# Gathered sums taken three behind each group, and a group of 128 ahead of the 512 gathered columns

## The chip, the cores and the metric

The kernel runs on one core of one Trainium2 chip. The metric is the device time of one execution in microseconds; the median of three runs of the kernel before is 3914.21 us (3911.45 to 3914.72). The profile is of one further execution.

## What is computed

A graph network on 6250 nodes with 128 features and 200,000 edges, sorted by destination. First comes a graph attention layer with a feed-forward part (not touched here), then four graph convolutions with the same edges; the change lies wholly in these. Cut to them, the reference is:

```python
def _gcn_conv(x, src, dst, W, b, n_nodes):
    h = x @ W
    s, d = concatenate([src, loops]), concatenate([dst, loops])
    deg = segment_sum(ones, d);  dis = rsqrt(deg)
    out = segment_sum(h[s] * (dis[s] * dis[d])[:, None], d)
    return out + b

h = relu(_batch_norm(_gcn_conv(x, src, dst, W1, b1), g1, be1))
h = relu(_batch_norm(_gcn_conv(h, src, dst, W2, b2), g2, be2))
h = relu(_gcn_conv(h, src, dst, W3, b3))
h = _gcn_conv(h, src, dst, W3, b3)
return x + h          # 6250 x 128, f32
```

Source and destination lists `s` and `d` hold the 200,000 edges and one loop per node. The sum over edges is linear, so the kernel takes most of it as a product with a matrix of edge counts.

## The kernel before

The nodes are 49 tiles of 128 (6272, padded). An earlier stage leaves a matrix of edge counts in device memory (`adj`, in strips of 32 destinations). The stage `convolutions` runs L = 4 layers. In each:

- **Start of a layer.** ScalarE rectifies `hT` into `cv_stage`, TensorE multiplies by W into `cv_w_ps`, ScalarE scales the rows into `cv_hs`, writes them to the table `hs_tab` and keeps a bf16 part; VectorE makes two more bf16 parts, so that three bf16 matmuls give close to f32. TensorE takes the parts of each piece at once into the first group's sum (`first_group`, L2304).
- **Dense groups.** A group is 512 destinations: 49 source tiles x 3 parts = 147 matmuls of 128x512 into one PSUM bank, `cv_acc` (`group`, L2290). The counts come from SP's queue (`counts_in`, L2012) in three chunks of 16, 16 and 17 source tiles. Each chunk has one buffer, which is refilled when the group before has used it (`cnt_used`), so a group's third chunk is asked for when the group before it ends. There are DG = 11 groups of 512 (0 to 10) for tiles 0 to 43, and one narrow group of 128 destinations for tile 44, with 147 matmuls of 128x128.
- **Gathered destinations.** For the last four tiles (45 to 48) there are no counts; each node there has a list of its sources in 56 slots. GpSimd gathers source rows from `hs_tab`, one indirect DMA per slot (L2063), in 28 batches of 8 slots through a ring of RING = 3 buffers; batch n waits until batch n - 3 has been summed. VectorE sums a batch with one TENSOR_REDUCE (`add_slots`, L2110). Seven batches are one tile. When a tile is complete, TensorE transposes it into `cv_acc` (`turn_sums`, L2375).
- **Reading a sum.** VectorE's `finish_group(i)` multiplies the bank by a row of scales (L2124), adds the bias into `hT` (L2128) and takes statistics (L2129). The list `SPANS` gives the 13 sums of a layer in order; two banks alternate by the index in it. After the last `finish_group` of a layer come the batch-norm coefficients (layers 0 and 1) and the next layer.
- **Last layer.** TensorE also transposes each finished sum back (`turn_rows`, L2368), VectorE adds `x` (`add_rows`, L2190), and SP writes it out (`rows_out`, L2019 and L2022). Two buffers `cv_hs` alternate, so `add_rows(n)` waits until the output DMA of n - 2 has landed.

The order on each engine is written out by hand, with waits on semaphores. Which batches are summed where is this loop on VectorE: 2 or 3 behind each of groups 0 to 10 (0, 2, 5, 7, 10, 12, 15, 17, 20, 22, 25, 28 in running total).

```python
for i in range(NGA):
    last = finish_group(i)
    if l == L - 1 and i:
        add_rows(i - 1)
    for b in range(NBK * min(i, DG) // DG, NBK * min(i + 1, DG) // DG):
        add_slots(b)
```

Of the kernel before, what the change touches and what calls it, by code (L numbers as in the profile page):

```python
# [13 lines left out]
P = 128  # L14
# [40 lines left out]
GRP = 512  # L55
# [14 lines left out]
SPARSE = 4  # L70
T0 = NT - SPARSE
# [2 lines left out]
PER_TILE = SLOTS // SB  # L74
NBK = SPARSE * PER_TILE
RING = 3
DG = T0 * P // GRP
LW = T0 * P - DG * GRP
ND = DG + 1
SPANS = [(i * (GRP // P), GRP // P) for i in range(DG)] + [(T0, SPARSE), (DG * (GRP // P), LW // P)]  # L80
NGA = len(SPANS)
CQ = ((0, 393), (393, 392), (785, 392), (1177, 392))

# [100 lines left out]
def settle(engine, steps_taken):  # L184

    engine.sem_inc(steps_taken, 1)
# [1723 lines left out]
def convolutions(nc, t, sb, pb, sem, g):  # L1910
# [8 lines left out]
    with ExitStack() as c:  # L1919
# [7 lines left out]
        SLOT_W = (SB + 1) * D  # L1927
        slots = [sb(f"cv_slots{r}", [P, SB + 1, D], F32, c) for r in range(RING - 1)]
        slots = [a[:] for a in slots]
# [23 lines left out]
        hs_out = [sem(f"cv_hs_out{u}") for u in range(2)]  # L1953
        slots_in = [sem(f"cv_slots_in{r}") for r in range(RING)]
        cnt_in = [sem(f"cv_cnt_in{q}") for q in range(3)]
# [3 lines left out]
        out_done = [sem(f"cv_out{u}") for u in range(2)]  # L1959
# [13 lines left out]
        @block.sync  # L1973
        def _(sp):
            flag = sp.value_load(irregular[0:1, 0:1], min_val=0, max_val=1)

            for l in range(L):

                with sp.If(flag):
                    sp.wait_ge(s["split"], (l + 1) * NW + 2)  # L1980
                    settle(sp, s["tick_sp"])
                    for r in range(3):
                        sp.dma_start(parts_tab.rearrange("(t p) (r d) -> p t r d", p=P, r=3)[:, :, r, :], parts[:, r, :, :]
                                     ).then_inc(s["table_out"], 16)
                    sp.wait_ge(s["table_out"], 48 * (l + 1))
                    settle(sp, s["tick_sp"])
                    with sp.Fori(0, NCH) as i:
                        sp.wait_ge(s["chunk_over"], l * NCH + i + 1)
                        settle(sp, s["tick_sp"])
                        sp.dma_start(six[:], src_pad[ds(i * P, P)].rearrange("(p c) -> p c", c=1)).then_inc(s["idx_in"], 16)  # L1990
                        sp.dma_start(dix[:], dst_pad[ds(i * P + FRONT, P)].rearrange("(p c) -> p c", c=1)
                                     ).then_inc(s["idx_in"], 16)
                    if l == L - 1:
                        with sp.Fori(0, NB // 2) as m:
                            for u in range(2):
                                sp.wait_ge(s["sum"], 2 * m + u + 3)
                                sp.dma_start(out[ds((2 * m + u) * BW, BW), :].rearrange("(b p) d -> p b d", p=P), hs[u][:]
                                             ).then_inc(out_done[u], 16)
                        sp.wait_ge(s["sum"], NB + 2)
                        sp.dma_start(out[(NB - 1) * BW:(NT - 1) * P, :].rearrange("(b p) d -> p b d", p=P),  # L2000
                                     hs[0][:, 0:BATCH - 1, :]).then_inc(out_done[0], 16)
                        sp.dma_start(out[(NT - 1) * P:N, :], hs[0][0:N_LAST, BATCH - 1, :]).then_inc(out_done[0], 16)
                        sp.wait_ge(out_done[0], 16 * (NB // 2 + 2))
                        sp.wait_ge(out_done[1], 16 * (NB // 2))
                with sp.Else():
                    def counts_in(i, n, width, strips):
                        for q, (b0, m) in enumerate(CHUNKS):
                            if isinstance(i, int) and l == 0 and i == 0 and q == 0:
                                sp.sem_inc(cnt_in[0], 16)
                                continue  # L2010
                            sp.wait_ge(cnt_used[q], n + 1)
                            sp.dma_start(cnt[q][:, 0:width, 0:m * SUB], adj[strips, :, b0 * SUB:(b0 + m) * SUB]  # L2012
                                         .rearrange("t p s -> p t s")).then_inc(cnt_in[q], 16)

                    def rows_out(n):
                        sp.wait_ge(s["sum"], n + 1)
                        t0, w = SPANS[n]
                        full = w if t0 + w < NT else w - 1
                        sp.dma_start(out[t0 * P:(t0 + full) * P, :].rearrange("(b p) d -> p b d", p=P),  # L2019
                                     hs[n % 2][:, 0:full, :]).then_inc(out_done[n % 2], 16)  # L2020
                        if full < w:
                            sp.dma_start(out[(NT - 1) * P:N, :], hs[n % 2][0:N_LAST, full, :]).then_inc(out_done[n % 2], 16)  # L2022
                    counts_in(0, l * ND, SPG, slice(0, SPG))
                    counts_in(1, l * ND + 1, SPG, slice(SPG, 2 * SPG))
                    if l < L - 1:
                        with sp.Fori(2, DG) as i:
                            counts_in(i, l * ND + i, SPG, ds(i * SPG, SPG))
                    else:
                        for i in range(2, DG):
                            counts_in(i, l * ND + i, SPG, slice(i * SPG, (i + 1) * SPG))  # L2030
                            if i >= LATE:
                                rows_out(i - LATE)
                    counts_in(DG, l * ND + DG, LW // SUB, slice(DG * SPG, DG * SPG + LW // SUB))
                    if l == L - 1:
                        for n in range(DG - LATE, NGA):
                            rows_out(n)
                        sp.wait_ge(out_done[0], 16 * 7)
                        sp.wait_ge(out_done[1], 16 * 7)

        @block.gpsimd  # L2040
        def _(pool):
# [11 lines left out]
            with pool.Else():  # L2053
                for l in range(L):
                    for u in range(2):
                        pool.wait_ge(hs_out[u], 16 * (NW // 2) * (l + 1))
                    for b in range(NBK):
                        n, (k, i) = l * NBK + b, divmod(b, PER_TILE)
                        if n >= RING:
                            pool.wait_ge(s["slots_used"], n - RING + 1)  # L2060
                        for e in range(SB):
                            at = i * SB + e
                            nc.gpsimd.indirect_dma_start(slots[n % RING][:, e, :], None, hs_tab[:, :],  # L2063
                                                         bass.IndirectOffsetOnAxis(slot_idx[:, k, at:at + 1], 0)
                                                         ).then_inc(slots_in[n % RING], 16)

        @block.vector
        def _(dve):
# [11 lines left out]
            for l in range(L):  # L2080
# [32 lines left out]
                def finish_group(i):  # L2113
                    u, n = i % 2, l * NGA + i
                    use = l * uses[u] + i // 2
                    t0, w = SPANS[i]
                    width, at = w * P, slice(t0 * P, (t0 + w) * P)
# [64 lines left out]
                with dve.Else():  # L2182
                    def add_rows(n):
                        t0, w = SPANS[n]
                        dve.wait_ge(s["out_ps"], n + 1)
                        if n >= 2:
                            dve.wait_ge(out_done[n % 2], 16 * (n // 2))
                        else:
                            dve.wait_ge(hs_out[n], 16 * (NW // 2) * L)
                        nc.vector.tensor_tensor(hs[n % 2][:, 0:w, :], x_sb[:, t0:t0 + w, :],  # L2190
                                                w_ps[n % 2][:, 0, 0:w * D].rearrange("p (b d) -> p b d", d=D), ALU.add
                                                ).then_inc(s["sum"], 1)

                    own_rows()
                    for i in range(NGA):
                        last = finish_group(i)
                        if l == L - 1 and i:
                            add_rows(i - 1)
                        for b in range(NBK * min(i, DG) // DG, NBK * min(i + 1, DG) // DG):
                            add_slots(b)  # L2200
                    if l < L - 1:
                        last.then_inc(s["y"], 1)
                    else:
                        add_rows(NGA - 1)
# [69 lines left out]
        def _(pe):  # L2274
# [36 lines left out]
            for l in range(L):  # L2311
# [43 lines left out]
                with pe.Else():  # L2355
# [6 lines left out]
                    def turn_rows(n):  # L2362
                        t0, w = SPANS[n]
                        pe.wait_ge(s["dch"], l * NGA + n + 1)
# [13 lines left out]
                    def next_group(i):  # L2378
                        pe.wait_ge(acc_read[i % 2], l * uses[i % 2] + i // 2 + 1)
                        if SPANS[i][0] == T0:  # L2380
                            turn_sums(acc[i % 2])
# [40 lines left out]
```

## Time and profile before

| | us |
|---|---|
| median of 3 runs | 3914.21 (3911.45 to 3914.72) |
| profiled execution, whole | 3912.45 |
| its span on the core | 3910.7 |
| convolutions, from about 2350 us to the end | about 1560 |
| TensorE busy over the whole span | 3568.2 (91%) |

The profiled execution is 1.76 us below the median and lies inside the runs. Its span is 1.75 us shorter than its own time. Busy shares cover stages with different limits; for this change only the last 1560 us count, and of these the end of each of the four layers (about 2722, 3109, 3496 and 3885 us) and the stretch in which gathers and dense groups run side by side.

### The profile page before, as it was taken

The numbers are of one execution on the slowest core, as the hardware profiler recorded it, in microseconds if no ns is written. First come the engines' busy times: TensorE is split into PE (matmuls) and PEld (weight loads), VectorE is DVE, ScalarE is ACT, GpSimd is POOL, SyncE is SP. The second block draws the span as 40 slices with busy tenths as digits, with TensorE's granted clock in tenths as the row PEclk, the third lists the DMA queues.
The fourth block names the chain that finished last, engine by engine and source line by source line (L and its number), as shares of the span: only waits on it lengthen the run. The fifth ranks groups of instructions, "written<-read, shape, count | busy, mean of one in ns | idle before, by whom it ended". The sixth has DMA issues, their size and how long they took to land. (4 is left out here: it accounts for less than half of the span.)

```text
span 3910.7 us, 61608 instructions
## 1 busy us (share of the span) xinstructions
PE 3568.2 (91%) x21338; PEld 2113.7 (54%) x21338; DVE 2412.0 (62%) x3535; ACT 1880.3 (48%) x5147; POOL 2355.3 (60%) x2509
## 2 busy tenths in 40 slices
PE   5799999999999999999995889999999999989998
PEld 4566666666666666666663544444544454444444
DVE  8798888888889888888884764222422242224222
ACT  4787888888878788787882563000200020002000
POOL 2677777777777777777772003655365546544654
PEclk8798888888889888888886999999999999999999
DMA  6443333333333343333335017876887688768885
GB/s 204 128 107 106 103 107 106 106 106 104 106 105 106 103 107 106 106 107 102 107 106 92 36 30 230 249 239 187 255 251 244 184 257 253 240 192 254 254 248 172
DMA packets 497047, 606.58 MB, mean 155 GB/s; under 512 B 60201, under 2 KB 427140, under 8 KB 496478
## 3 DMA queue, kind: packets, MB, share of 16 engines
q1 hardware_dynamic: 358950, 341.00, 28.9%
q0 software_dynamic: 79968, 166.57, 17.4%
q10 hardware_dynamic: 57848, 95.46, 6.9%
q8 instruction: 151, 2.47, 0.3%
q14 instruction: 130, 1.06, 0.1%
HBM read 488.30 MB, written 116.12 MB: 155 GB/s over the span
## 5 line engine op out<-in xcount | busy, mean ns | idle before, releaser
L917 POOL DMA_INDIRECT fts<-ft_tab,src_all x1568 | 1479.5, 944 | 477.7 <-issue 477.4
L2290 PE MATMUL cv_acc<-cv_cnt,cv_parts 128*128 128x512 bf16 (+1 forms) x6468 | 1312.6, 367 | 0.0
L2290 PEld LDWEIGHTS cv_acc<-cv_cnt,cv_parts 128*128 128x128 bf16 x6468 | 616.6, 99 | 692.0
L2063 POOL DMA_INDIRECT cv_slots<-hs_tab,slot_idx x600 | 567.5, 946 | 473.0 <-issue 176.6
L954 DVE TENSOR_TENSOR ohk<-iota_ps,key_cols 128x784 bf16<-128x784 f32 x784 | 725.5, 967 | 6.1
L2124 DVE TENSOR_TENSOR cv_y<-cv_acc,dis_row 128x512 f32<-128x512 f32 (+1 forms) x52 | 34.4, 661 | 950.2 <-PE cv_acc L2290 924.4
L1047 ACT ACTIVATE dist_l<-lo_iota,low 128x128 bf16<-128x128 f16 x1960 | 593.7, 387 | 18.6 <-ACT low L1042 0.8
L1206 PE MATMUL agg_ps<-terms,oh 128*64 128x141 f32 x2744 | 530.5, 365 | 28.8 <-DVE terms L991 27.9
L1206 PEld LDWEIGHTS agg_ps<-terms,oh 128*64 128x64 f32 x2744 | 459.8, 181 | 84.1 <-DVE terms L991 71.3
L1099 ACT CAST strip<-adj_ps 128x392 bf16<-128x392 f32 x784 | 371.9, 474 | 275.2 <-PE adj_ps L1150 246.5
L1150 PE MATMUL adj_ps<-ohk,ohl 128*128 128x196 bf16 x3136 | 430.1, 262 | 0.0
L2063 POOL DMA_INDIRECT spare<-hs_tab,slot_idx x296 | 279.6, 945 | 212.1 <-issue 87.4
L968 DVE TENSOR_TENSOR prod<-ftd_ps,fts 128x780 f32<-128x780 f32 (+1 forms) x392 | 271.4, 692 | 214.2 <-DMA fts<-ft_tab,src_all 204.7
L1172 PE MATMUL ftd_ps<-win,ohdT 64*128 64x130 f32 x3136 | 313.7, 324 | 48.2 <-DVE prod L968 47.1
L1146 PE MATMUL adj_ps<-own,own_low 32*128 32x392 bf16 x784 | 269.8, 344 | 75.1 <-DVE ohk L954 46.4
L2259 ACT ACTIVATE cv_sd<-cv_mv,eps 128x1 f32<-128x1 f32 x2 | 0.6, 294 | 697.4 <-DVE cv_tmp L2210 697.4
L1150 PEld LDWEIGHTS adj_ps<-ohk,ohl 128*128 128x128 bf16 x3136 | 235.0, 101 | 180.2 <-issue 178.4
L1172 PEld LDWEIGHTS ftd_ps<-win,ohdT 64*128 64x128 f32 x3136 | 234.2, 210 | 137.1 <-DVE prod L968 71.5
L1054 ACT ACTIVATE ohl<-dist_l 128x1280 bf16<-128x1280 bf16 x196 | 248.9, 1270 | 18.4 <-ACT dist_l L1047 0.7
L991 DVE TENSOR_TENSOR terms<-fts,most_ps 128x1040 f32<-128x1040 f32 x196 | 241.1, 1230 | 10.1 <-ACT most_ps L1078 9.8
L1004 DVE TENSOR_REDUCE score<-prod 128x80 f32<-128x1040 f32 x196 | 242.4, 1237 | 6.7
L949 DVE TENSOR_TENSOR ohl<-iota_ps,low_cols 128x768 bf16<-128x768 f32 x196 | 185.8, 948 | 0.0
(287 smaller groups left out, 3271.4 us busy)
## 6 DMA issues: line engine op xcount, KB each, us to landing
cv_cnt<-adj SPq DMA_DIRECT2D x88, 2048.0 KB, 9.3
cv_cnt<-adj SPq DMA_DIRECT2D x44, 2176.0 KB, 9.3
adj<-strip ACTq DMA_DIRECT2D x196, 392.0 KB
fts<-ft_tab,src_all POOLq DMA_INDIRECT x1568
win<-ft_tab SPq DMA_DIRECT2D x196, 65.0 KB
hs_tab<-cv_hs ACTq DMA_DIRECT2D x24, 448.0 KB, 3.8
cv_slots<-hs_tab,slot_idx POOLq DMA_INDIRECT x600
agg_tab<-res SPq DMA_DIRECT2D x196, 35.2 KB
```

Of the source, the lines that this page charges most:

```text
L917: nc.gpsimd.indirect_dma_start(fts[u][:, k, :], None, ft_tab[:, :], bass.IndirectOffsetOnAxis(src_all[:, n, k:k + 1], 0)).then_inc(gathere ...
L954: nc.vector.tensor_tensor(ohk[:, k.s, at, :], key_no.unsqueeze(1).to_broadcast([P, QC, KEYS]), columns(key_cols, k)[:, at].unsqueeze(2).to ...
L968: nc.vector.tensor_tensor(by_half(prod[:]), ftd_ps[:, :, 0:n * HD].rearrange("p a (c f) -> p a c f", f=HD), by_half(fts[k.f][:]), ALU.mult ...
L1047: last = nc.scalar.activation(dist_l[:, n, :], lo_iota[:], ACT.Abs, bias=low[:, k.s, n:n + 1], scale=-1.0)
L1054: nc.scalar.activation(ohl[:, k.s, LD:NA * SC, :], dist_l[:], ACT.Relu, bias=1.0, scale=-1.0).then_inc(ohl_done, 1)
L1099: nc.scalar.copy(strip[:, k.s, :, QS * q:QS * (q + 1), :].rearrange("p t a d -> p a t d"), adj_ps[q % 2][:, 0:QS * KEYS].rearrange("p (a t ...
L1146: nc.tensor.matmul(adj_ps[q % 2][:, 0:QS * KEYS], own_low[:, P - SUB - SUB * k.u:2 * P - SUB - SUB * k.u], tile_of, start=True, stop=False)
L1150: last = nc.tensor.matmul(adj_ps[q % 2][:, a * KEYS:(a + 1) * KEYS], ohl[:, k.s, n, :], ohk[:, k.s, n, :], start=False, stop=(a == QS - 1 ...
L1172: last = nc.tensor.matmul(ftd_ps[:, half, m * HD:(m + 1) * HD], ohdT[at, k.u, (c0 + m) * P:(c0 + m + 1) * P], win[at, k.u, :], start=True, ...
L1206: nc.tensor.matmul(agg_ps[0:WD, 0:WA], oh[:, k.o, col, half, :], terms[:, k.s, n, :], start=(n == 0), stop=False)
L2063: nc.gpsimd.indirect_dma_start(slots[n % RING][:, e, :], None, hs_tab[:, :], bass.IndirectOffsetOnAxis(slot_idx[:, k, at:at + 1], 0)).then ...
L2290: last = nc.tensor.matmul(a[:, 0:width], parts[:, r, b, :], cnt[q][:, 0:width // SUB, (b - b0) * SUB:(b - b0 + 1) * SUB], start=(b == 0 an ...
```

## The change

The narrow group comes before the gathered tiles in `SPANS`, and VectorE sums three batches behind each of groups 0 to 8 and the 28th behind group 9; none behind group 10. The final waits on the two output semaphores follow the new places (the gathered tiles, with two output DMAs, now have an even index).

```diff
+PER_GROUP = 3
-SPANS = [(i * (GRP // P), GRP // P) for i in range(DG)] + [(T0, SPARSE), (DG * (GRP // P), LW // P)]
+SPANS = [(i * (GRP // P), GRP // P) for i in range(DG)] + [(DG * (GRP // P), LW // P), (T0, SPARSE)]
...
-                        sp.wait_ge(out_done[0], 16 * 7)
-                        sp.wait_ge(out_done[1], 16 * 7)
+                        sp.wait_ge(out_done[0], 16 * 8)
+                        sp.wait_ge(out_done[1], 16 * 6)
...
-                        for b in range(NBK * min(i, DG) // DG, NBK * min(i + 1, DG) // DG):
+                        for b in range(min(NBK, PER_GROUP * i), min(NBK, PER_GROUP * (i + 1))):
                             add_slots(b)
```

On TensorE, at the end of a layer that is not the last (the 512-wide rows are groups 9 and 10, the 128x128 x147 row is the narrow group, `cv_acc<-ident,spare` the turning of the gathered sums, `cv_w_ps` the next layer's products), before:

```order
L2290 MATMUL cv_acc<-cv_cnt,cv_parts 128x512 x147
L2386 REGISTER_ALU
L2386 COMPARE_AND_BRANCH
L2375 MATMUL cv_acc<-ident,spare 128x128 x4
L2290 MATMUL cv_acc<-cv_cnt,cv_parts 128x128 x147
L2355 UNCONDITIONAL_BRANCH
L2317 MATMUL cv_w_ps<-cv_W,cv_stage 128x128 x7
```

and now (all lines are one further down):

```order
L2291 MATMUL cv_acc<-cv_cnt,cv_parts 128x512 x147
L2387 REGISTER_ALU
L2387 COMPARE_AND_BRANCH
L2291 MATMUL cv_acc<-cv_cnt,cv_parts 128x128 x147
L2376 MATMUL cv_acc<-ident,spare 128x128 x4
L2356 UNCONDITIONAL_BRANCH
L2318 MATMUL cv_w_ps<-cv_W,cv_stage 128x128 x7
```

The four transposes have moved behind the narrow group. On VectorE, the end of the last layer from the multiply of group 10 on (`cv_hs<-x_sb,cv_w_ps` adds `x`), before:

```order
L2124 TENSOR_TENSOR cv_y<-cv_acc,dis_row 128x512
L2128 TENSOR_SCALAR hT<-cv_y,cv_bias 128x512
L2129 BN_STATS cv_stats<-hT 128x6
L2190 TENSOR_TENSOR cv_hs<-x_sb,cv_w_ps 128x512
L2110 TENSOR_REDUCE spare<-cv_slots 128x128
L2110 TENSOR_REDUCE cv_slots<-spare 128x128
L2110 TENSOR_REDUCE spare<-cv_slots 128x128
L2124 TENSOR_TENSOR cv_y<-cv_acc,dis_row 128x512
```

and now:

```order
L2125 TENSOR_TENSOR cv_y<-cv_acc,dis_row 128x512
L2129 TENSOR_SCALAR hT<-cv_y,cv_bias 128x512
L2130 BN_STATS cv_stats<-hT 128x6
L2191 TENSOR_TENSOR cv_hs<-x_sb,cv_w_ps 128x512
L2125 TENSOR_TENSOR cv_y<-cv_acc,dis_row 128x128
L2129 TENSOR_SCALAR hT<-cv_y,cv_bias 128x128
L2130 BN_STATS cv_stats<-hT 128x6
L2191 TENSOR_TENSOR cv_hs<-x_sb,cv_w_ps 128x512
L2125 TENSOR_TENSOR cv_y<-cv_acc,dis_row 128x512
```

The three sums behind group 10 are gone from there, the narrow sum is read next, and the gathered 512 last. TensorE in the last layer, before:

```order
L2290 MATMUL cv_acc<-cv_cnt,cv_parts 128x512 x147
L2368 MATMUL cv_w_ps<-ident,hT 128x128 x4
L2375 MATMUL cv_acc<-ident,spare 128x128 x4
L2368 MATMUL cv_w_ps<-ident,hT 128x128 x4
L2290 MATMUL cv_acc<-cv_cnt,cv_parts 128x128 x147
L2368 MATMUL cv_w_ps<-ident,hT 128x128 x5
```

and now:

```order
L2291 MATMUL cv_acc<-cv_cnt,cv_parts 128x512 x147
L2369 MATMUL cv_w_ps<-ident,hT 128x128 x4
L2291 MATMUL cv_acc<-cv_cnt,cv_parts 128x128 x147
L2369 MATMUL cv_w_ps<-ident,hT 128x128 x4
L2376 MATMUL cv_acc<-ident,spare 128x128 x4
L2369 MATMUL cv_w_ps<-ident,hT 128x128 x5
```

The last row's five transposes were four of the gathered tiles and then the narrow one; now the narrow one comes first and the four last.

## Rows read from the trace of the kernel before

**Rows 1.** Waits: waiter <- releaser: us in total, times, longest.

```profile
PE cv_acc L2375 <- DVE spare L2110: 32.3, 4, 8.2
```

**Rows 2.** Chain that ended last, layer 2: start us, us, what.

```profile
3179.12 317.29 PE cv_acc L2290 x1470
3496.43 0.70 DVE cv_y L2124
...
3502.51 2.09 DVE spare L2110
...
3505.12 10.17 PE cv_acc L2290 x147
3516.82 0.72 PE cv_w_ps L2317 x4
```

**Rows 3.** Timeline, VectorE, end of layer 2: start, us, instruction, [idle before].

```profile
3505.16 0.69 DVE L2124 TENSOR_TENSOR cv_y<-cv_acc,dis_row 128x512 f32<-128x512 f32 x1 [0.57 <-PE cv_acc L2375]
...
3506.41 0.67 DVE L2129 BATCH_NORM_STATS2 cv_stats<-hT 128x6 f32<-128x490 f32 x1
3515.32 0.29 DVE L2124 TENSOR_TENSOR cv_y<-cv_acc,dis_row 128x128 f32<-128x128 f32 x1 [8.24 <-PE cv_acc L2290]
...
3515.97 0.29 DVE L2129 BATCH_NORM_STATS2 cv_stats<-hT 128x6 f32<-128x128 f32 x1
```

**Rows 4.** Timeline, VectorE, ends of layers 0 and 1.

```profile
2721.76 0.69 DVE L2124 TENSOR_TENSOR cv_y<-cv_acc,dis_row 128x512 f32<-128x512 f32 x1 [23.41 <-PE cv_acc L2290]
...
2740.59 0.29 DVE L2124 TENSOR_TENSOR cv_y<-cv_acc,dis_row 128x128 f32<-128x128 f32 x1 [8.16 <-PE cv_acc L2290]
...
3109.33 0.69 DVE L2124 TENSOR_TENSOR cv_y<-cv_acc,dis_row 128x512 f32<-128x512 f32 x1 [23.39 <-PE cv_acc L2290]
...
3129.01 0.29 DVE L2124 TENSOR_TENSOR cv_y<-cv_acc,dis_row 128x128 f32<-128x128 f32 x1 [8.79 <-PE cv_acc L2290]
```

**Rows 5.** Windows: stretch, us, PE PEld DVE ACT POOL busy (count), PEclk, DMA, GB/s.

```profile
3505.00:3508.00 3.00, 3.00 (x30) 3.00 (x29) 1.85 (x3) 0.00 (x0) 0.00 (x0) 0.50 0.00 0
3510.00:3515.00 5.00, 5.00 (x93) 5.00 (x91) 0.00 (x0) 0.00 (x0) 0.00 (x0) 1.00 0.86 264
...
3134.00:3137.00 3.00, 2.90 (x13) 2.70 (x14) 1.44 (x4) 2.46 (x7) 0.00 (x0) 0.50 1.10 348
```

**Rows 6.** The page's DMA issues of counts: KB each, median us to landing.

```profile
cv_cnt<-adj SPq DMA_DIRECT2D x88, 2048.0 KB, 9.3
```

**Rows 7.** DMA issues from 3480 to 3540 us: the narrow group's third chunk.

```profile
cv_cnt<-adj SPq DMA_DIRECT2D x1, 544.0 KB, 4.0
```

**Rows 8.** Timeline, GpSimd: layer 2's first gather.

```profile
3171.70 0.94 POOL L2063 DMA_INDIRECT spare<-hs_tab,slot_idx  x1 [59.95 <-DMA hs_tab<-cv_hs]
```

**Rows 9.** Timeline, VectorE, layer 2, behind groups 0 and 1.

```profile
3186.93 2.16 DVE L2110 TENSOR_REDUCE cv_slots<-spare 128x128 f32<-128x1152 f32 x1 [5.32 <-DMA spare<-hs_tab,slot_idx]
3197.06 2.14 DVE L2110 TENSOR_REDUCE cv_slots<-cv_slots 128x128 f32<-128x1152 f32 x1 [7.97 <-DMA cv_slots<-hs_tab,slot_idx]
3210.88 0.69 DVE L2124 TENSOR_TENSOR cv_y<-cv_acc,dis_row 128x512 f32<-128x512 f32 x1 [11.68 <-PE cv_acc L2290]
```

**Rows 10.** Timeline, all engines, end of the last layer.

```profile
3884.92 0.60 PE L2368 MATMUL cv_w_ps<-ident,hT 128*128 128x128 f32 x4
...
3885.12 0.69 DVE L2124 TENSOR_TENSOR cv_y<-cv_acc,dis_row 128x512 f32<-128x512 f32 x1 [23.25 <-PE cv_acc L2290]
...
3896.42 0.67 DVE L2190 TENSOR_TENSOR cv_hs<-x_sb,cv_w_ps 128x512 f32<-128x512 f32 x1
...
3907.02 0.39 SPq L2022 DMA_DIRECT2D out<-cv_hs  x1
3907.45 0.38 SPq L2019 DMA_DIRECT2D out<-cv_hs  x1
```

**Rows 11.** DMA issues from 3880 to 3911 us: the output.

```profile
out<-cv_hs SPq DMA_DIRECT2D x3, 256.0 KB, 3.6
```

**Rows 12.** The page's DMA issues: the output over the whole span.

```profile
out<-cv_hs SPq DMA_DIRECT2D x11, 256.0 KB, 9.7
```

## The prediction

> **What bounds the kernel now.** I read the waits first, then the chain that ended last, then the timeline and the clock at the four layer ends. TensorE is the bound inside a layer: ten groups of 512 follow each other in 317.29 us without a gap, 31.73 us each [rows 2]. Its one wait that belongs to this change is the turning of the gathered sums, which waits for VectorE's last batch in each of the four layers, 32.3 us in all and 8.2 at the longest [rows 1]. The chain shows why it lies on the path: when group 10 ends (call that moment T; 3496.43 us in layer 2), VectorE reads the sum, then sums three batches, the last from 3502.51 for 2.09 us; only then do the last transpose and, behind it in TensorE's order, the narrow group come (10.17 us from 3505.12), and the next layer's products wait for the last read [rows 2]. The windows show a second cost. TensorE starts the narrow group at a granted clock of 0.50, the lower level (1.2 GHz), after some 8 us without work: 30 matmuls in 3 us, 100 ns each. At 1.00 (2.4 GHz) the same matmuls take 5 us for 93, 53.8 ns each [rows 5].
>
> **Layers 0 to 2, what goes and what comes.** The three batches behind group 10 go ahead of it, to a place where VectorE has more than 20 us of idle time in a group (the read of group 10 came after 23.41 us of idle in layer 0 [rows 4]). Nothing then stands between group 10 and the narrow group: its bank is that of group 9, read 31 us before. I take its 147 matmuls at 53.8 ns, because TensorE comes from an uninterrupted group at full clock: 7.9 us. The bound on the other side is the 10.17 us that it takes now [rows 2, 5].
>
> Its counts must be there. Chunks 0 and 1 are asked for when group 10 has used 16 and 32 of its 49 source tiles, 21 and 11 us before T. Chunk 2 (544 KB) is asked for at T and needed after 96 matmuls, at T + 5.2; it landed 4.0 us after its issue [rows 7]. So that hides, with 1.2 us to spare. It hid before behind the sums too, which is why the trace does not show a wait for it.
>
> Behind the narrow group, TensorE turns the four gathered tiles: four transposes of this shape took 0.60 us [rows 10]. VectorE meanwhile reads the narrow sum: from 3515.32 to 3516.26, 0.94 us [rows 3]. Then it reads the gathered 512 columns: from 3505.16 to 3507.08, 1.92 us [rows 3]. This is an addition to the path; before, it was hidden behind the narrow group. The end of the layer is now T + 7.9 + 0.94 + 1.92, with joints of 0.05, that is T + 10.8. It was T + 19.8 in layer 2 (3516.26 - 3496.43) [rows 2, 3], and by the same reading (2740.59 - 2721.76 and 3129.01 - 3109.33, plus 0.94) T + 19.8 in layer 0 and T + 20.6 in layer 1 [rows 4]. Gains: 9.0, 9.8 and 9.0, together 27.8 us.
>
> The next layer's start stays as it is in its order, and its counts are asked for some 2.5 us earlier relative to the layer's end than before, since the narrow group releases its chunks earlier. I count this at nothing; SP's queue holds nothing else there. One cost may be new: between layers 2 and 3 TensorE now idles about 3 us instead of 1.5, and might fall to the lower level, as it stands between layers 1 and 2, where 13 matmuls filled 2.90 of 3 us at 0.50 [rows 5]. At full clock they would have taken half, so at most 1.5 us, and less where ScalarE is the slower one. I take 0 and keep 1.5 for the range.
>
> The Trainium skill ("TensorE: Matmul & The Clock Gate", Part 1) states two clock levels, 1.2 GHz after idle time and 2.4 GHz after work, with 106.7 and 55.6 ns from start to start at 128 columns; the trace agrees, with 100 and 53.8 ns. By that figure the narrow group would take 8.2 us. The Trainium skill (same title, Part 4, on transposes) also says that transposes do not count as work for this gate; the four that now end a layer would then lengthen the idle time by 0.6 us, and the sum would be smaller by up to the 1.5 us of the bound above. No run here shows it yet.
>
> **Three batches behind every group.** The gathers must keep up. In layer 2 they start at 3171.70 [rows 8] = T - 324.7; the first batch was summed at 3186.93 and the second at 3197.06, both as they landed, so a batch takes 10.1 us, and a sum 2.15 us [rows 9]. Three need 30.4 us against 31.73 of a group [rows 2]. The tightest place is the first: the third batch lands at about 3207.2, its sum ends at 3209.4, and the read of group 1 is due at 3210.88 [rows 9]. If it were late, nothing would be lost until 31 us later, since group 2 uses the other bank. Later the distance grows by 1.3 us a group. The last batch lands at T - 324.7 + 15.2 + 27 x 10.1 = T - 36.8, waits for group 9 and is summed by T - 28. The transposes want it at T + 7.9, so the cover is 36 us. GpSimd already ran at this pace beside full count traffic between groups 0 and 3, and TensorE's groups there were no longer. Cost: nothing.
>
> **Last layer.** T is 3885.12 [rows 10]. The transposes of group 9 (0.60 us, from T - 0.2) come first, so the narrow group ends at T + 8.3. VectorE reads it until T + 9.2 and adds `x` to group 10 (0.67 us [rows 10]) until T + 9.9; the output of group 10 is issued and lands 3.6 us later [rows 11], at T + 13.5. Beside this run the read of the gathered 512 (to T + 11.9), the narrow output, and four transposes (to T + 12.5). The last addition needs the buffer of group 10: it is a new wait, from about T + 12.5 to T + 13.6. Then 0.67 us and two issues of 0.39 and 0.38 us [rows 10] end at T + 15.1. Before, the last issue ended at 3907.83 = T + 22.7, with 2.9 us to the span's end, and I leave that tail as it is. Gain 7.6 us. A landing of 9.7 us, the median over the whole span where transfers compete [rows 12], would make it 1.5; a landing below 2.5 us would make it 8.7. I take the value of the last 31 us, since nothing else is in flight there.
>
> **Sum.** 27.8 + 7.6 = 35.4 us. The profiled execution took 3912.45 us and would take 3877.1; the median of the runs is 1.8 us above the profiled one, so I forecast 3879 us for the median (-0.9%).
>
> **Rivals.** (A) The order helps but the clock does not: the narrow group still takes 10.2 us (10.9 in layer 1, where the half level lasted longer). That takes back 2.3, 3.0, 2.3 and 1.9 us, 9.5 in all: gain 25.9, time 3888. For: the clock fell at different distances from the start of idle time. Against: no gap is left in front of the group. (B) Chunk 2 comes late and takes the place of the wait: if it landed like the large chunks, in 9.3 us [rows 6], the narrow group would end at T + 9.3 + 51 x 0.0538 = T + 12.0, 4.1 us later in each layer: gain 19, time 3895. Against: 544 KB is a quarter of a large chunk and was measured at 4.0 alone; the gathers that ran beside it are gone. (C) The last output buffer costs 6 us more: gain 29.3, time 3885. (D) Slower: the gathers fall behind. One place, the transposes behind the narrow group, and one price: with p us for a batch the last sum ends at T - 324.7 + 5.1 + 28p + 2.15, and it decides once that passes T + 7.9 plus the gain of 9 us, at p = 11.9 us. At p = 12.5, which is 2.4 more than measured, each layer would lose 15 us net: 3914 + 60 = 3974. For: every batch now goes at this pace and the gathers get no pause. Against: the measured 10.1 is set by the issue of eight DMAs and was the same beside full count traffic. (E) The change does nothing: TensorE waits for something else at T: 3914. The order of the instructions speaks against it.
>
> **Numbers.** Forecast 0.72 (own range 3873 to 3884), A 0.09, B 0.05, C 0.07, D 0.03, E 0.02, and 0.02 for smaller losses beside E. The bound of 1.5 us and the three runs' spread of 3.3 us are in the forecast's range; widened to A and C, and to the low side because the layer starts may profit from earlier counts, it is 3870 to 3890. What counts as a change here is 0.2%, 7.8 us. Faster: 0.72 + 0.09 + 0.05 + 0.07 + 0.01 = 0.94; same 0.03; slower 0.03.
>
> **What would show it.** Right: at each layer end the narrow group starts at T at a granted clock of 1.00 and ends at T + 7.9; the wait for VectorE at L2376 is gone; the last read ends at T + 10.8; no reduce lies behind group 10; the last gather of a layer is issued more than 30 us before T. Wrong in a step: a gap near T + 5 inside the narrow group (B); a rate of 100 ns in it (A); a wait for the output DMA over 3 us in the last addition (C); TensorE waiting for a reduce at L2376 or for a late read at groups 2 or 3 (D). I would be wrong altogether if the ten groups of 512 in a layer took longer than 317 us.

## The result, and the profile after

The changed kernel takes 3877.86 us (median of 4 runs, 3875.01 to 3881.62), the kernel before 3912.83 us on the same chip (4 runs, 3910.61 to 3914.72). The ratio is 0.9911, with a 95% interval of 0.9894 to 0.9929. The forecast was 3879 us.

The table follows four stretches of the convolutions in the two profiled executions. T is VectorE's first read of group 10; "start" runs from the last read of a layer to the first read of the next one.

| us | before | after | less by |
|---|---|---|---|
| whole span | 3910.7 | 3873.5 | 37.2 |
| up to the first read of layer 0 | 2404.55 | 2401.59 | 3.0 |
| groups 0 to 10, a layer | 317.21, 317.21, 317.21, 321.13 | 317.21, 317.20, 317.20, 321.13 | 0.0 |
| T to the next layer's first read | 70.36, 69.89, 67.56 | 61.59, 61.75, 58.57 | 8.8, 8.1, 9.0 |
| of it from T to the end of the last read | 19.8, 20.6, 19.8 | 11.0, 11.0, 11.0 | 8.8, 9.6, 8.9 |
| of it the start | 50.6, 49.3, 47.7 | 50.6, 50.8, 47.6 | 0.0, -1.5, 0.1 |
| last layer, T to the end of the span | 25.6 | 17.3 | 8.3 |

So 34.2 us come from the four layer ends, and 3.0 us of this pair of executions from stages that the change doesn't touch; those moved between 2400.5 and 2410.3 us over all the profiled executions here and are chance. The medians differ by 35.0.

The chain that ended last, at the end of layer 2 (start, us, what), answers to [rows 2]:

```profile
3159.23 325.50 PE cv_acc L2291 x1617
3485.69 0.60 DVE cv_y L2125
3486.32 0.50 DVE hT L2129
3486.84 0.68 DVE cv_stats L2130
3488.07 0.72 PE cv_w_ps L2318 x4
```

The reader is to see one piece of 1617 matmuls (eleven groups of 147, the narrow one among them) where there were 1470, a break with three sums, and 147. The chain now leaves TensorE only for the read of the gathered columns. The timeline of the same moment (start, us, instruction) answers to [rows 3]:

```profile
3475.70 9.02 PE L2291 MATMUL cv_acc<-cv_cnt,cv_parts 128*128 128x512 bf16 x150
...
3476.54 0.69 DVE L2125 TENSOR_TENSOR cv_y<-cv_acc,dis_row 128x512 f32<-128x512 f32 x1 [27.75 <-PE cv_acc L2291]
...
3484.55 0.61 PE L2376 MATMUL cv_acc<-ident,spare 128*128 128x128 f32 x4
3484.75 0.29 DVE L2125 TENSOR_TENSOR cv_y<-cv_acc,dis_row 128x128 f32<-128x128 f32 x1 [6.27 <-PE cv_acc L2291]
...
3485.61 0.67 DVE L2125 TENSOR_TENSOR cv_y<-cv_acc,dis_row 128x512 f32<-128x512 f32 x1
```

The narrow sum is ready at T + 8.21, the gathered one is read from T + 9.07. The waits list has no entry for L2376 any more. The windows (stretch, us, busy PE PEld DVE ACT POOL with counts, granted clock, DMA share, GB/s) answer to [rows 5]: the narrow group at full clock, and the start of layer 2 at half of it.

```profile
3478.00:3484.00 6.00, 6.00 (x112) 6.00 (x110) 0.48 (x1) 0.00 (x0) 0.00 (x0) 1.00 0.90 284
...
3112.00:3119.00 7.00, 6.22 (x29) 5.99 (x29) 2.47 (x6) 5.50 (x12) 0.00 (x0) 0.50 1.12 356
```

The last batch of layer 2: GpSimd's last gather, and VectorE's sum of it, which ends 27.7 us before T (the first row is GpSimd's, the second VectorE's):

```profile
3431.16 0.94 POOL L2064 DMA_INDIRECT spare<-hs_tab,slot_idx  x1 [0.30 <-issue]
```

```profile
3446.67 2.12 DVE L2111 TENSOR_REDUCE spare<-spare 128x128 f32<-128x1152 f32 x1
```

In the last layer the chain shows the new wait for the buffer of group 10's output, as [rows 10] did not have:

```profile
3856.64 8.22 PE cv_acc L2291 x147
...
3865.75 0.68 DVE cv_hs L2191
...
3866.44 2.29 DMA out<-cv_hs
...
3868.82 0.69 DVE cv_hs L2191
```

The output landed in 2.29 us, and VectorE waited 0.39 us for it beyond its own work.

### The profile page after: what moved, and what is told of

The parts are those of the page before. It is cut to its first block and busy times, and to the rows that moved or that the text cites. A ratio compares the mean times of both kernels' runs of the same rounds, so it can differ in the third digit from the quotient of the medians.

```text
span 3873.5 us, 61608 instructions
## 1 busy us (share of the span) xinstructions
PE 3554.9 (92%) x21338; PEld 2105.3 (54%) x21338; DVE 2411.6 (62%) x3535; ACT 1881.1 (49%) x5147; POOL 2358.9 (61%) x2509
## 5 line engine op out<-in xcount | busy, mean ns | idle before, releaser
L2291 PEld LDWEIGHTS cv_acc<-cv_cnt,cv_parts 128*128 128x128 bf16 x6468 | 608.5, 98 | 692.4
L1147 PE MATMUL adj_ps<-own,own_low 32*128 32x392 bf16 x784 | 269.5, 344 | 76.9 <-DVE ohk L955 49.5
L2111 DVE TENSOR_REDUCE spare<-cv_slots 128x128 f32<-128x1152 f32 x43 | 91.4, 2126 | 165.1 <-DMA cv_slots<-hs_tab,slot_idx 164.9
```

Source lines behind the costliest of these rows:

```text
L1147: nc.tensor.matmul(adj_ps[q % 2][:, 0:QS * KEYS], own_low[:, P - SUB - SUB * k.u:2 * P - SUB - SUB * k.u], tile_of, start=True, stop=False)
L2291: last = nc.tensor.matmul(a[:, 0:width], parts[:, r, b, :], cnt[q][:, 0:width // SUB, (b - b0) * SUB:(b - b0 + 1) * SUB], start=(b == 0 an ...
```

## Experiments

Medians stand with their number of runs. Since the stages ahead scatter by some us from run to run, and the stretches from T on repeat within 0.2 us between executions of one kernel, the stretches are the finer measure; both are given. The order of the four numbers is always: T to the next layer's first read for layers 0, 1 and 2, and T to the end for the last. Before: 70.4, 69.9, 67.6, 25.6. Changed kernel: 61.6, 61.8, 58.6, 17.3.

### The changed kernel again, and each part alone

> The changed kernel once more, beside the others on the same chip. My theory (the three sums leave TensorE's path at each layer end, and the narrow group runs at full clock): 34 us below the kernel before, 3876 to 3881. The theory that part of the first difference was chance in the stages ahead of the convolutions (3.0 us of 37.2 in the two profiled executions): the same number, with those stages within 1 us of before.

3875.76 us (4 runs) against 3911.34 (14 runs), ratio 0.9907 (0.9892 to 0.9922). Stretches 61.6, 61.8, 58.4, 17.2. The first read of layer 0 came at 2409.17 us here and at 2401.59 in the first profile: 7.6 us of chance in the stages ahead, so the 3.0 us above can be that. The expectation that these stages stay within 1 us of the kernel before did not hold: they were 4.6 us later here. It is the four stretches that repeat.

The order alone:

```diff
-                        for b in range(min(NBK, PER_GROUP * i), min(NBK, PER_GROUP * (i + 1))):
+                        for b in range(NBK * min(i, DG) // DG, NBK * min(i + 1, DG) // DG):
```

> Only the narrow group is moved ahead of the gathered tiles; the sums stay spread 2 or 3 behind groups 0 to 10, three of them behind group 10. Theory 1 (the order alone is enough): these three end at T + 8.2, just when the narrow group ends, so they hide behind it; the last read ends at T + 11.0 to 11.5 as in the changed kernel, the time is 3878 to 3881. Theory 2 (the earlier sums carry the gain): the transposes still wait for VectorE, the layer end stays near T + 17 or later, time 3900 or more.

3878.44 us (5 runs), ratio 0.9913 (0.9899 to 0.9926). Stretches 61.7, 61.9, 58.6, 17.6, that is 0.6 us more than the changed kernel in all. Its timeline at the end of layer 2, with T at 3475.66:

```profile
3481.89 2.15 DVE L2111 TENSOR_REDUCE spare<-spare 128x128 f32<-128x1152 f32 x1
3483.67 0.75 PE L2376 MATMUL cv_acc<-ident,spare 128*128 128x128 f32 x4
3483.96 0.28 DVE L2125 TENSOR_TENSOR cv_y<-cv_acc,dis_row 128x128 f32<-128x128 f32 x1
```

The last of the three sums ends at T + 8.4, the narrow group at T + 8.2. The narrow sum is read 0.1 us later than in the changed kernel there and in layer 0, and 0.35 to 0.4 us later in layer 1 and in the last layer, where the three sums end at T + 8.6 and T + 9.1. Theory 1 stands, and the earlier sums add next to nothing to the new order.

The sums alone, in the kernel before:

```diff
+PER_GROUP = 3
-                        for b in range(NBK * min(i, DG) // DG, NBK * min(i + 1, DG) // DG):
+                        for b in range(min(NBK, PER_GROUP * i), min(NBK, PER_GROUP * (i + 1))):
```

> Only the sums are moved (three behind each group, none behind group 10); the gathered tiles stay ahead of the narrow group. Theory 1 (either part alone removes the wait, and this one has the shorter tail, since the small sum is read last): the four transposes take 0.5 us at T, the narrow group ends at T + 8.7, the last read at T + 9.7 against T + 11.0 in the changed kernel; in the last layer the last output is 64 KB and waits for no buffer, about 2 us better. Gain 41 us, time 3871 to 3874, below the changed kernel. Theory 2 (the order is what matters): no better than 3878, or the wait at L2375 remains.

3871.93 us (4 runs), ratio 0.9901 (0.9886 to 0.9916). Stretches 60.7, 59.6, 57.8, 15.8: 5.3 us less than the changed kernel. Its timeline at the end of layer 2, with T at 3474.09:

```profile
3473.89 0.60 PE L2376 MATMUL cv_acc<-ident,spare 128*128 128x128 f32 x4
...
3474.84 8.38 PE L2291 MATMUL cv_acc<-cv_cnt,cv_parts 128*128 128x128 bf16 x147 [0.35 <-DVE cv_y L2125]
...
3483.25 0.29 DVE L2125 TENSOR_TENSOR cv_y<-cv_acc,dis_row 128x128 f32<-128x128 f32 x1 [5.41 <-PE cv_acc L2291]
```

The transposes stand ahead of the narrow group and cost 0.95 us there (with a wait of 0.35 us for the other bank), but the last read is the short one: it starts at T + 9.2 and ends at T + 10.1, against T + 11.0. The forecast of T + 9.7 left out the wait for the bank, which is read only after T. Of the 5.3 us, 2.6 are this earlier end of the last read in layers 0 to 2 (0.87 us each), 1.45 are the last layer, and 1.3 are the start of layer 2 (49.5 us here, 50.8 in the changed kernel), which no run explains.

It was run once more beside the changed kernel:

> The kernel with only the sums moved, once more, beside the changed kernel on one chip. Theory 1 (its tail is shorter by 1.3 us in each of three layers and by 1.5 us in the last): 4 to 6 us below the changed kernel. Theory 2 (the difference in the first runs was chance): the same time within 2 us.

> The changed kernel as the partner of the run before it: 3876 to 3880, 34 us below the kernel before, both theories.

3873.75 us (4 runs) against 3874.65 (4 runs) of the changed kernel: 0.9 us, and not the 4 to 6 of theory 1. Stretches 60.7, 59.6, 57.8, 15.9 against 61.6, 61.8, 58.6, 17.2: again 5.3 us less in the trace. Over both pairs of runs the medians are 3872.5 and 3875.2 us (8 runs each). In whole times the difference is inside the scatter of the stages ahead; the difference in the trace repeats to 0.1 us. By the trace this is the best kernel here; whole times do not separate the two.

### The clock by itself

In the kernel before, the idle time is filled (FILL = 33) and nothing else is changed:

```diff
                         for k in range(SPARSE):
+                            if k == SPARSE - 1:
+                                for f in range(FILL):
+                                    nc.tensor.matmul(w_ps[0][:, 1, :], parts[:, 0, 0, :],
+                                                     parts[:, 0, 0:4, :].rearrange("p b d -> p (b d)"), start=True, stop=True)
                             pe.wait_ge(s["slots_used"], l * NBK + (k + 1) * PER_TILE)
```

> The kernel before, with 33 matmuls of 128x512 into an unused PSUM bank while TensorE waits for the last gathered sum (7.1 us of the 8.2 us wait). Nothing is taken off the path; only the idle time is filled. Theory 1 (the granted clock carries part of the gain): the narrow group runs at 1.00 and takes 8.2 us in place of 10.2, 10.9, 10.2 and 9.6, gain 8 us, time 3905. Theory 2 (the clock is a reading without an effect on the time, and the whole gain is the wait): 3913, no change. If the filler itself is late it can only add up to 1 us a layer.

3901.93 us (10 runs), ratio 0.9977 (0.9968 to 0.9986), 9.4 us below before. Stretches 67.6, 68.7, 66.1, 23.8: 7.2 us less. The narrow group behind the filler, in the timeline and by windows:

```profile
3493.44 7.07 PE L2377 MATMUL cv_w_ps<-cv_parts 128*128 128x512 bf16 x32
...
3501.59 8.37 PE L2291 MATMUL cv_acc<-cv_cnt,cv_parts 128*128 128x128 bf16 x147
```

```profile
3496.00:3500.00 4.00, 4.00 (x20) 1.84 (x19) 3.93 (x3) 0.00 (x0) 0.00 (x0) 1.00 0.18 65
3502.00:3507.00 5.00, 5.00 (x93) 5.00 (x91) 1.64 (x3) 0.00 (x0) 0.00 (x0) 1.00 0.27 67
```

The clock stays at 1.00 through the wait, and the narrow group takes 8.4 us in place of 10.2. The wait itself is as long as before. The narrow groups alone gave back 8.3 us in the four layers; the layer starts took 1.0 of it again. So of the 34 us about 7 are the clock, and some 27 the wait, after what the read of the gathered columns adds to the path; theory 2 falls.

### How far the gathers were from their limit

GpSimd gets small extra work behind each batch, four or eight iotas (PAD):

```diff
+                        for e in range(PAD):
+                            nc.gpsimd.iota(iota[:], [[1, P]], base=0, channel_multiplier=0,
+                                           allow_small_or_imprecise_dtypes=True).then_inc(padded, 1)
+                            pool.wait_ge(padded, n * PAD + e + 1)
```

> The changed kernel with four small iotas on GpSimd behind each batch of gathers, each waited for, so that a batch takes longer (about 11.3 us in place of 10.1; p is read from the trace). Theory 1 (the gathers have a cover of 36 us, used up only at p = 11.4 for the transposes at T + 8.2, with the last sum at T - 317.5 + 28p): no group and no layer end moves, T to the next layer's first read stays 61.6, 61.8, 58.6 and 17.3 us. Theory 2 (the pace is already at its limit, since VectorE waits for the landing of nearly every batch): each 1.2 us shows in full, 28 x 1.2 = 34 us a layer, over 100 us in all.

One run, 3876.92 us; stretches 61.6, 61.7, 58.7, 17.2, nothing moved. The pace went from 10.0 to 11.35 us a batch (11.5 in the mean of layer 2, since two batches took longer). The last sum of layer 2, with T at 3478.07, ends 1.0 us before T where it ended 27.7 us before T in the changed kernel:

```profile
3474.91 2.13 DVE L2117 TENSOR_REDUCE spare<-spare 128x128 f32<-128x1152 f32 x1 [7.35 <-DMA spare<-hs_tab,slot_idx]
```

> The same with eight iotas, p about 12.5 us. Theory 1: now beyond the point. The last sum ends at about T' - 317.5 + 28p with T' the end of group 10 had nothing moved, T' + 32.5 at p = 12.5, so each layer is 24 us longer than in the changed kernel and the whole about 97 us longer (about 3975, above the kernel before). Some groups of 512 wait for a bank, since VectorE reads them late. Theory 2 (pace at its limit from the start): twice the cost of the run with four iotas. Theory 3 (GpSimd's pace does not matter): 3878.

One run, 3986.36 us, above the kernel before. At 12.6 us a batch (12.7 in the mean of layer 2), the last sum of layer 2 ends here:

```profile
3570.86 2.08 DVE L2117 TENSOR_REDUCE spare<-spare 128x128 f32<-128x1152 f32 x1 [12.42 <-DMA spare<-hs_tab,slot_idx]
```

Group 0 was read at 3220.08 and would have been followed by T 317.2 us later, at 3537.3; the sum ends 35.7 us behind that. TensorE also waits for banks that VectorE reads late, in the waits list (waiter, releaser, us, times, longest):

```profile
PE cv_acc L2297 <- DVE cv_y L2131: 51.2, 11, 8.8
```

From the first read of one layer to that of the next it is 28.1, 27.4 and 28.1 us more than in the changed kernel, and 22.3 in the last layer, 106 in all against 97 expected; the expectation counted 12.5 us a batch, and 0.1 us more for each of 28 batches is 2.8 us a layer. Theory 1 stands on these two runs: no cost at 11.35 us a batch, and nearly the full price at 12.6, so the point lies between. That VectorE waits for the landing of 72 of the 112 batches in the changed kernel costs nothing.

### A late third chunk

```diff
+                            if q == 2 and width < SPG:
+                                sp.dma_start(cnt[q][:, 0:SPG, 0:m * SUB], adj[DG * SPG:DG * SPG + SPG, :, b0 * SUB:(b0 + m) * SUB]
+                                             .rearrange("t p s -> p t s")).then_inc(cnt_in[q], 16)
+                                continue
```

> The changed kernel, where the narrow group's third chunk of counts is loaded at the full width of 16 strips (2176 KB in place of 544 KB), of which the group uses the same part as before. Theory 1 (the third chunk is asked for at T and covered only because it is small: needed at T + 5.4): it lands at about T + 9, the narrow group ends at T + 12, each layer loses 3.5 to 4.5 us, 3892 to 3896 in all. Theory 2 (the counts have a cover that the trace does not show, or arrive ahead): 3878, no change.

3902.64 us (6 runs), ratio to before 0.9972 (0.9959 to 0.9984). Stretches 67.9, 66.3, 63.9, 21.8: 20.7 us more than the changed kernel, above the 14 to 18 expected. The profiled execution is the fastest of the six, and the medians differ by more: 3902.64 against 3874.65 to 3877.86 us for the changed kernel. The waits list and a window inside the narrow group of layer 2, behind the wait:

```profile
PE cv_acc L2295 <- DMA cv_cnt<-adj: 14.6, 4, 4.8
```

```profile
3498.00:3500.00 2.00, 2.00 (x22) 2.00 (x20) 0.00 (x0) 0.00 (x0) 0.00 (x0) 0.51 1.11 348
```

In layer 2 the wait is 3.7 us as worked out, and in the four layers 4.8, 3.4, 3.7 and 2.8. But the clock fell in the wait (layers 0 and 2) or up to 1 us behind it (layer 1 and the last), and the 51 matmuls that remained ran at the half clock for all or part of their time: 4.4 to 5.6 us, where they take 2.8 at full clock. The mechanism of rival B is real; it did not happen in the changed kernel, where the chunk is a quarter as large. The clock at the time of a short wait was left out of the expectation.

### The starts of the layers

20, 20 and 10 filler matmuls behind the transposes of the changed kernel, and 14, 14 and 5 behind the narrow group of the kernel with the sums alone:

```diff
                         next_group(DG + 1)
+                        for f in range(FILL[l]):
+                            nc.tensor.matmul(w_ps[0][:, 1, :], parts[:, 0, 0, :],
+                                             parts[:, 0, 0:4, :].rearrange("p b d -> p (b d)"), start=True, stop=True)
```

> The kernel with the sums moved alone (gathered tiles still ahead of the narrow group), and 14, 14 and 5 matmuls of 128x512 into an unused bank at the ends of layers 0, 1 and 2, in TensorE's idle time before the next layer's products. Theory 1 (the half clock at a layer's start costs little, as ScalarE and the DMAs limit it): T to the next first read 60.7, 59.6 and 57.8 us as without them, within 1 us each. Theory 2 (it costs half of the 4 to 9 us for which it lasts): 2 us or more less in two of the three.

One run, 3878.03 us; stretches 60.1, 60.2, 57.8, 15.9 against 60.7, 59.6, 57.8, 15.8 without them. One start is 0.6 us shorter, one 0.6 longer: theory 1.

> The changed kernel with 20, 20 and 10 matmuls of 128x512 into an unused bank behind the transposes of layers 0, 1 and 2, so that TensorE's idle time before the next layer is filled. In the changed kernel the granted clock was 0.50 for some 9 us at the start of layer 2, and that start took 1.5 us longer than before (T to the next first read 61.75 us). Theory 1 (the half clock there is the cause of these 1.5 us): 60.3 us after layer 1, and at most 0.5 us less after layers 0 and 2. Theory 2 (the phase of the table writes against the count loads is the cause): 61.3 or more.

One run, 3882.73 us; stretches 61.1, 61.2, 58.4, 17.2. The clock stayed at 1.00 through the start of layer 2:

```profile
3114.00:3122.00 8.00, 6.75 (x38) 3.88 (x37) 4.08 (x13) 2.62 (x6) 0.00 (x0) 1.00 1.10 350
```

61.2 lies between the 60.3 of theory 1 and the 61.3 of theory 2. The filler took 0.6 us off that start, and the other 0.9 of the 1.5 us is not explained. Nor is it shown that the 0.6 are the clock: in the kernel with the sums alone the same kind of filler made this start 0.6 us longer. With filler it takes 50.1 and 50.2 us in the two kernels. Without, it takes 49.3 (before) and 49.5 us (sums alone), with the clock at 0.50 for about 3.5 us, and 50.8 us in the changed kernel, with 0.50 for about 10 us. The DMA share there is 1.10 with the filler and 1.12 without, and the table writes share it with the count loads, but no run took these apart.

## Why the prediction was right

- **The wait leaves the path.** Predicted from T + 19.8, 20.6 and 19.8 to T + 10.8; measured T + 11.0 in all three. Either part of the change would have done it: the order alone hides the three sums behind the narrow group, to 0.1 to 0.4 us, and the sums alone have them done before T. The prediction treated the two as one cause and did not see that they overlap, nor that the order costs 0.9 us a layer against leaving it.
- **The narrow group at full clock.** Predicted 7.9 us from 53.8 ns a matmul, measured 8.21 us, 55.8 ns. The window's count of 93 in 5 us holds matmuls cut by its edges, so the rate from it was 4% too fast. The group ends 0.3 us later than predicted in each layer, but the last read of layers 0 to 2 only 0.2. The figure of the Trainium skill ("TensorE: Matmul & The Clock Gate", Part 1), 55.6 ns, was the closer one.
- **Chunk 2 of the counts.** Predicted to land in time, with 1.2 us to spare; there is no wait for counts in the trace after, and the run with the large chunk shows what a miss costs.
- **The gathers.** Predicted pace 10.1 us, last sum at T - 28 us; measured 10.0 us and, in layer 2, an end at T - 27.7 (it started at 3446.67, took 2.12, and T is 3476.54). The predicted turning point of 11.9 us a batch lies between the two runs at 11.35 and 12.6 that bracket it. The cost of zero was right.
- **The starts.** Counted at nothing, with up to 1.5 us kept for a lower clock between layers 2 and 3. The clock did fall there (0.50 from 3489 us), and that start took 47.6 us against 47.7: nothing. Whether the four transposes ahead of it had a part in that fall, no run separates. The 1.5 us came at the start of layer 2 instead, which the prediction held unchanged; the cause is open.
- **The last layer.** Predicted 7.6 us, measured 8.3. The output landed in 2.29 us and not in the 3.6 that the last 31 us of the trace before had as a median; this was the lower bound of the prediction, not its value. The read of the narrow sum ran 0.35 us later, with the narrow group, and took part of this gain back.
- **Rivals.** A (no gain from the clock) is refuted by the 8.21 us of the narrow group in the trace after, and by the filler in the kernel before. B and D are real mechanisms that did not set in; D gave a kernel slower than before once forced (one run). C did not happen, with 0.39 us of wait in place of 6. E is refuted by the waits.

The sum was 35.4 us; the four stretches give 34.2 and the medians 35.0. The sum came closer than its terms, since their misses partly cancelled: 0.5 us less at the ends of layers 0 to 2, 1.4 us less at the starts behind them, 0.7 us more in the last layer. That the medians differ by 35.0 is within the chance of the stages ahead.

## What to carry to other kernels

When a change has two parts that each remove the same wait, run each alone: here the sums without the new order are 5 us better in the trace. Most of it comes from the shorter last read at the end of each layer; 1.3 us are not explained. A wait on TensorE of some us costs more than its length, since the work behind it begins at half clock; filling it with work that nobody reads gave 7 us here while the wait stayed. The cover of a background engine is a number with a cliff behind it: 14% more time for each batch of gathers cost nothing, 26% cost 106 us (one run each).

## What the runs showed of the hardware that was not expected

- The clock fell about 3 us into a wait of 3.7 us (late chunk, layer 2), and did not fall within the 2.9 us of idle time before layer 3's first products in the changed kernel but about 1 us behind their beginning. In the kernel before it fell 2.1 to 5.4 us after TensorE had stopped, at the four layer ends.
- At half clock for 7 us at the start of layer 2, TensorE was busy for 6.22 of them, and the run that kept the clock up was only 0.6 us shorter there. A busy share near 90% at half clock did not mean that the clock set the time of this stretch.
